# Thirty-six unread TensorE products at the end of the key stage

## The reference

```python
q = (x @ Wq + bq); kv = cond @ Wkv + bkv          # x here is layer_norm(x)
q, k = _fq_sym(q * scale, axis=-1), _fq_sym(k, axis=-1)
v = _fq_sym(v, axis=2)
attn = softmax(einsum('bhqd,bhkd->bhqk', q, k))    # all 2048 rows against all 4096 keys
out = einsum('bhqk,bhkd->bhqd', _fq_unsigned(attn, axis=-1), v)
x = x + tanh(g_xattn[0]) * (out @ Wp + bp)
x = x + tanh(g_ffn[0]) * ffn(layer_norm(x))        # bitlinear, silu, gelu, layer norm, bitlinear
```

## Time and profile before

| | |
|---|---|
| three runs | 1759.59, 1753.40, 1759.55 us; median 1759.55 |
| the profiled execution | 1753.62 us |
| its span, first to last instruction | 1751.8 us |
| mean granted clock of TensorE | 0.968 |
| VectorE busy in the span | 1625.9 us (93%) |
| TensorE, ScalarE, GpSimd busy | 1536.5, 1398.5, 1312.2 us |

### The profile page before, as it was taken

How to read it: one execution, slowest core, us unless ns; L and a number is a source line. 1 busy time by engine, 2 the same in 40 slices (tenths; PEclk the granted TensorE clock), 3 DMA queues, 4 the chain that set the end, 5 groups by cost and what they waited for, 6 DMA issues and landing times.

```text
span 1751.8 us, 34664 instructions
## 1 busy us (share of the span) xinstructions
PE 1536.5 (88%) x13207; PEld 752.4 (43%) x13207; DVE 1625.9 (93%) x2210; ACT 1398.5 (80%) x1354; POOL 1312.2 (75%) x1315
## 2 busy tenths in 40 slices
PE   7989968898898889988889898988888888988996
PEld 3544423444444444444444444444444444433332
DVE  6969879999999999999999999999999999489887
ACT  4568878888898888889888888987888887777874
POOL 1157646898989889898988988898999998454332
PEclk9999987999999999999999999999999998889998
DMA  7578858999958999986898989698898876214223
GB/s 244 195 243 290 282 185 157 165 187 170 163 110 148 181 168 184 173 160 113 146 182 172 184 171 158 113 149 155 148 160 146 161 137 142 73 36 96 58 70 84
DMA packets 721031, 274.22 MB, mean 157 GB/s; under 512 B 675609, under 2 KB 680281, under 8 KB 719586
## 3 DMA queue, kind: packets, MB, share of 16 engines
q1 hardware_dynamic: 719058, 268.81, 74.7%
q0 software_dynamic: 704, 1.62, 0.3%
q10 hardware_dynamic: 1104, 1.57, 0.2%
HBM read 68.21 MB, written 35.95 MB: 59 GB/s over the span
## 4 chain that ended last, share of the span: by engine, by line
DVE 52%; PE 13%; POOL 10%; issue 7%; ACT 2%; DMA 1%; POOLq 0%; DVEq 0%; ACTq 0%; SPq 0%
DVE att_scaled L1756 50%; POOL att_probsT L1455 7%; PE att_scores L1185 3%; PE att_ps_o L1205 2%; PE att_scores L1125 2%; PE att_scores L1145 2%; ACT att_pairs L1282 1%; PE att_scores L1186 1%; POOL att_low_row L1445 1%; DMA att_pairsT<-att_pairs 1%; DVE att_v_largest L1725 1%; PE att_scores L1085 1%; POOL att_bias_row L1448 0%; PE att_ps_v L1205 0%; POOL layer_o_sum L1503 0%
## 5 line engine op out<-in xcount | busy, mean ns | idle before, releaser
L1756 DVE TENSOR_SCALAR_CACHE_REDUCE att_scaled<-att_scores,layer_nsq 128x1536 f32<-128x1536 f32 (+1 forms) x768 | 1201.3, 1633 | 12.2 <-PE att_scores L1145 11.1
L1282 ACT ACTIVATE att_pairs<-att_scaled,att_bias_row 128x4096 uint8<-128x4096 f32 x256 | 950.4, 3713 | 123.9 <-DMA att_pairsT<-att_pairs 79.0
L1455 POOL CAST att_probsT<-att_pairsT 128x2048 bf16<-128x2048 uint8 x512 | 953.7, 1891 | 94.3 <-DMA att_pairsT<-att_pairs 81.7
L1145 PE MATMUL att_scores<-first_head_area 96*128 96x512 bf16 x1024 | 298.2, 396 | 91.8 <-DVE att_scaled L1756 77.0
L1145 PE MATMUL att_scores<-att_head_area 96*128 96x512 bf16 x1024 | 289.3, 385 | 66.2 <-DVE att_scaled L1756 63.2
L1104 PEld LDWEIGHTS att_ps_o<-att_v_head,att_probsT 128*128 128x128 bf16 x8192 | 242.8, 96 | 64.4 <-issue 5.2
L1104 PE MATMUL att_ps_o<-att_v_head,att_probsT 128*128 128x32 bf16 x8192 | 245.1, 176 | 2.1 <-ACT layer_o_sum L1273 2.0
L1145 PEld LDWEIGHTS att_scores<-first_head_area 96*128 96x128 bf16 x1024 | 81.7, 99 | 253.3 <-DVE att_scaled L1756 171.7
L1145 PEld LDWEIGHTS att_scores<-att_head_area 96*128 96x128 bf16 x1024 | 79.6, 97 | 214.6 <-DVE att_scaled L1756 153.4
L1085 PE MATMUL att_scores<-att_head_area 96*128 96x512 bf16 x621 | 169.6, 382 | 0.0
L1085 PE MATMUL att_scores<-first_head_area 96*128 96x512 bf16 x570 | 157.4, 386 | 0.0
(11 more groups left out here) (188 smaller groups left out, 1615.3 us busy)
## 6 DMA issues: line engine op xcount, KB each, us to landing
layer_w2T<-ctx_T SPq DMA_DIRECT2D x96, 256.0 KB, 3.9
k_rows<-pre_shared SPq DMA_DIRECT2D x32, 392.0 KB, 3.1
kv_weights_ctx_in<-in_ctx_dram SPq DMA_DIRECT2D x32, 256.0 KB, 3.8
ctx_T<-layer_o_sum SPq DMA_DIRECT2D x8, 1024.0 KB, 5.9
pre_w_more<-in_L_ffn_w_dram SPq DMA_DIRECT2D x18, 256.0 KB, 3.2
pre_x_in<-in_x_dram SPq DMA_DIRECT2D x16, 256.0 KB, 4.7
pre_xb<-in_x_dram SPq DMA_DIRECT2D x16, 256.0 KB, 3.7
xb<-pre_xb SPq DMA_DIRECT2D x16, 256.0 KB, 3.4
```

The lines of the kernel that those rows point to most:

```text
L1145: last = pe.matmul(buffer[:, x:x + 512], q_head[slot][:, at:at + P], k_head[slot][:, STARTS[j] + x:STARTS[j] + x + 512], start=True, stop= ...
L1282: act.activation(pairs[g % R_BUFS][:, :].bitcast(U8).rearrange("p (c two) -> p two c", two=2), scaled[u][:, :].rearrange("p (two c) -> p t ...
L1455: pool.tensor_copy(probsT[g % C_BUFS][:, parity * HALF:(parity + 1) * HALF, :].rearrange("p k q -> p (k q)"), bytes_now.rearrange("p (n tw ...
L1756: dve.tensor_scalar(scaled[u][:, STARTS[j]:STARTS[j] + WIDTHS[j]], scores[(g * NCH + j) % 2][:, 0:WIDTHS[j]], kept["nsq"][:, g:g + 1], Non ...
```

## The change

Behind the last step of the key stage, and before the barrier, TensorE gets 36 products of a 128x128 bf16 identity by 512 columns of bf16 (`q_int[0]`, the integers of a query tile, which nobody needs any more). They are written to one PSUM bank, `ps_in[0]`, which nothing reads again. They wait for nothing and signal nothing.

```diff
         ROUND_LAG = 3
+        UNREAD = 36
...
                 for g in range(3, STEPS):
                     step(g)
+                spare = ps_in[0][:, :, :].rearrange("p k q -> p (k q)")
+                for _ in range(UNREAD):
+                    pe.matmul(spare, kept["identb"][:, :], q_int[0][:, :], start=True, stop=True)
```

## The result

| | before | after |
|---|---|---|
| runs | 1753.40 to 1760.55 us, median 1759.59 (5 runs) | 1766.37 to 1771.37 us, median 1770.09 (5 runs) |
| ratio after / before | | 1.0056, 95% interval 1.0036 to 1.0076 |
| profiled execution | 1753.62 us, span 1751.8 | 1769.84 us, span 1768.0 |
| VectorE idle ahead of its chunks | 12.2 us | 25.0 us |

The change costs 10 us. The forecast was 1759.2 in a range of 1752 to 1762, so it was wrong. The two profiled executions are 16.2 us apart, since the one of before is one of its two shortest; the medians are 10.5 us apart.

A forecast was written before the change was run, and what follows sets the result against it. The prediction took VectorE in the attention stage as the bound. Hidden products cost 0 and the clock gave 0 to -0.1 us: 1753.5 us on the profiled execution; with 0.1 to 0.4 off, the median was 1759.2 us, range 1752 to 1762.

The forecast's parts named there:

- What bounds the kernel: Attention stage: VectorE, 52% of the span; a faster TensorE could give at most 11.1 us there.
- The 36 products, 7.9 us to 248.6, hidden by the barrier: End of key stage: products run from 240.7 to 248.6, 5.1 us ahead of the barrier's release at 253.7.
- the eight rows of 3.60 us: End of key stage: read as eight f32 products at full clock, about 0.43 us apart, ending at 240.84.
- The clock falls again, between 250.1 and 253.95; sum 0 to -0.1: Before the attention stage: the clock likely falls again, only later, and the stage starts at 0.50; 0 to -0.1 us.
- Cost: 0: At the barrier: the added products cost nothing, since no other engine waits for them and the bank is not read.
- The ring's step: Attention stage, unit 16: VectorE gives its early gain back to ScalarE's ring of three buffers, leaving 0.7 of 4.2 us.
- A small shift is made larger by the transfers: First head: a start shifted by tenths may meet transfers otherwise; median between 1753.4 and 1762; chance 8%.
- Products longer than their cover: At the barrier: products outlast their cover; isolated 1768.6 median (2%), half clock +1.6 us (3%); chance 5%.
- The two levels of before, 6 us apart: Whole kernel before: quick executions at 1753.4 and 1753.62, the other two runs at 1759.6, cause unknown.

The follow-up runs named there:

- the third experiment: 18 f32 products of 128x512 added at the change's place, against the kernel before: median 1772.2 us, ratio 1.0059 (1.0044 to 1.0075).

## Why the prediction was wrong

- *What bounds the kernel*: right. A microsecond counts where VectorE waits, and 12.8 of the 16.2 us between the two profiled executions are such waits.
- *The 36 products, 7.9 us to 248.6, hidden by the barrier*: right; they end near 248.4, with 5.1 us to spare. One reading was wrong without harm: the eight rows of 3.60 us at the end of the key stage are four f32 products, two instructions each. It did harm in the third experiment, which I built on it.
- *The clock falls again, between 250.1 and 253.95; sum 0 to -0.1*: right; it fell near 252.8, and the first 30 us are as they were.
- *"Cost: 0"* is the step that failed. I counted the products' time and who waits for them, and took it that nothing else moved. The runs showed in its place a loss of 10 us in the attention stage that comes with 72 more instructions ahead of it, whatever their work. They moved TensorE's instruction fetch against the units of the stage: by 2.5 us at its first packet, 3.7 us by the estimate above. Its packets run on the transfer engines that the ring needs, and ScalarE's waits for transfers grew from 79 to 122 us. The row with the 105 packets stood on the page, and I didn't read it.
- *The ring's step* said where it could show: ScalarE starts an exponential each 4.98 us in head 0 against VectorE's 4.69, and three buffers are used up by unit 16. The right use of it was as a warning: a ring so close to its limit can turn tenths of a us per transfer into waits. I used it only to take away from a gain.
- *The rivals.* "A small shift is made larger by the transfers" (8%) was the right family, with the wrong cause (a start shifted by tenths), too small a size (up to 1762) and the sign left open. "Products longer than their cover" gave nearly the right time, 1768.6, by a mechanism that isn't there.
- *The two levels of before, 6 us apart*, are not borne out: the 35 executions of before on one later chip fill the range from 1754.6 to 1769.5 us without a gap of that kind. What spreads them isn't shown.

What is shown: the loss hangs on the count of TensorE instructions ahead of the stage and not on their work at this place; of the shifts tried, 72 and 328 = 256 + 72 harm, and 4, 128, 192 and 256 don't; the packets move with the count and come back to their place after 256; transfers of the ring that share time with a fetch packet land later, the more so if it comes late in them, and the kernels with the loss have more of these. The last link, that the packets are what makes those transfers slower, rests on this agreement alone: I found no way to move packets without moving instructions. Open is why the packets fall late in more transfers after a shift of 72 than after 4, 128, 192 or 256.

## What to carry to other kernels

Instructions can have a cost of their own, apart from their time: here they shifted the engine's instruction fetch for all that followed, in a kernel with a tight ring of transfers. A result of half a per cent after an edit on an engine with a long program should be tried again with the count padded (here to 256 instructions, 128 products) before the edit is credited or blamed. An edit's count is to be read in the trace, not in the source: an f32 product counted twice here. And unread work ahead of a stage keeps the clock only so far: in this kernel it brought the stage a full clock for its first 3 us and 0.63 us of VectorE's time.

## What the runs showed of the hardware that I had not expected

TensorE's instructions came in packets of 16.4 KB, about 256 products and loads apart, some 13 us here; one took 1.0 us of one transfer engine, and the transposing transfers under way landed 0.7 to 1.1 us later (4.54 to 4.60 us without, 5.3 to 5.6 with). An f32 product of 128x512 was two matrix instructions with a weight load each, 0.43 us apart (36 in 15.61 us). The delays from the last product to the fall of the clock were between 1.5 and 5.35 us in the kernel before and some 4.4 us in the changed one (248.4 to 252.8).
